# A CIN tower with 39 fields: layer 0's last pair tile as one float32r matmul

## The reference, cut to what matters

```python
prev = x                                          # [512, 39, 16]
for k in range(3):
    h = prev.shape[1]                             # 39, 128, 128
    z = jnp.einsum('bmd,bhd->bdmh', x, prev).reshape(b, D, m * h)
    t = jnp.einsum('bdc,co->bdo', z, ws[k]) + bs[k]      # co: o = 128
    t = jnp.transpose(t, (0, 2, 1))
    norm = jnp.sqrt(jnp.sum(t * t, axis=(-2, -1), keepdims=True))
    t = t / norm
    logit.append(t); prev = t
```

## Time and profile before

| | |
|---|---|
| median of 3 runs | 1101.58 us (1101.01 to 1102.05) |
| the profiled execution | 1101.28 us, span 1099.6 us |
| TensorE matmul busy | 96% |
| VectorE busy | 88% |
| GpSimd busy | 79% |
| ScalarE busy | 71% |
| mean DMA traffic | 37 GB/s |

### The profile page before, as it was taken

The page is one execution under the profiler, slowest core; times in us unless marked ns, Lnnn a source line. Parts: engine busy times, 40 slices in busy tenths (PEclk is TensorE's granted clock), DMA queues, the critical chain, the costliest instruction groups (busy, mean ns, idle before and its releaser), DMA issues.

```text
span 1099.6 us, 17904 instructions
## 1 busy us (share of the span) xinstructions
PE 1052.5 (96%) x4394; PEld 794.1 (72%) x4394; DVE 969.0 (88%) x3317; ACT 780.5 (71%) x2628; POOL 866.9 (79%) x726
## 2 busy tenths in 40 slices
PE   0798999999999999999999999999999999999999
PEld 0366687777778787777778777777777777788773
DVE  2467799998999999999999999999999999899892
ACT  3266586877768687776868777786868777688762
POOL 5587798888889888888888888888888888577660
PEclk9899999999999999999999999999999999999999
DMA  6503040110303011030303002030301203000000
GB/s 228 131 13 73 2 118 7 35 41 3 73 3 73 2 35 42 5 71 3 73 2 71 5 11 66 3 73 2 74 2 20 56 3 73 0 2 1 1 1 1
DMA packets 56735, 41.20 MB, mean 37 GB/s; under 512 B 37915, under 2 KB 40859, under 8 KB 56502
## 3 DMA queue, kind: packets, MB, share of 16 engines
q1 hardware_dynamic: 49145, 32.17, 12.5%
q10 hardware_dynamic: 2365, 6.60, 1.7%
q0 software_dynamic: 5120, 1.29, 1.3%
HBM read 38.09 MB, written 1.94 MB: 36 GB/s over the span
## 4 chain that ended last, share of the span: by engine, by line
PE 67%; POOL 21%; issue 6%; ACT 4%; DMA 1%; DVE 0%; SPq 0%; POOLq 0%; ACTq 0%
POOL sums L333 17%; PE bank_a L554 10%; PE bank_d L554 9%; PE acc L619 9%; PE bank_d L555 9%; PE bank_d L556 9%; PE bank_a L556 9%; PE bank_a L555 9%; POOL gathered L320 4%; ACT scaled L441 2%; PE turned L595 1%; ACT sums L441 1%; PE bank_a L684 1%; DMA x_pairs<-x_scratch 1%; PE bank_d L708 1%
## 5 line engine op out<-in xcount | busy, mean ns | idle before, releaser
L333 POOL TENSOR_TENSOR sums<-sums,scaled 128x512 f32<-128x512 f32 (+1 forms) x512 | 642.8, 1256 | 154.0 <-ACT scaled L441 119.3
L756 DVE SCALAR_TENSOR_TENSOR sums<-bank_d,x_col,sums 128x128 f32<-128x128 f32 x2304 | 654.8, 339 | 74.4 <-PE bank_d L556 58.8
L441 ACT ACTIVATE scaled<-bank_a,x_col 128x128 f32<-128x128 f32 x1920 | 550.6, 382 | 152.9 <-PE bank_a L556 144.4
L554 PE MATMUL bank_d<-w_hi,prev_lo 128*128 128x512 f32 x640 | 286.1, 447 | 1.2 <-DVE sums L775 0.9
L554 PE MATMUL bank_a<-w_hi,prev_lo 128*128 128x512 f32 (+1 forms) x640 | 274.5, 429 | 12.0 <-POOL prev_lo L338 6.3
L556 PE MATMUL bank_d<-w_hi,prev_hi 128*128 128x512 f32 x640 | 253.3, 396 | 0.0
L555 PE MATMUL bank_d<-w_lo,prev_hi 128*128 128x512 f32 x640 | 253.0, 395 | 0.0
L556 PE MATMUL bank_a<-w_hi,prev_hi 128*128 128x512 f32 (+1 forms) x640 | 246.2, 385 | 0.0
L555 PE MATMUL bank_a<-w_lo,prev_hi 128*128 128x512 f32 (+1 forms) x640 | 245.9, 384 | 0.0
L441 ACT ACTIVATE sums<-bank_a,x_col 128x128 f32<-128x128 f32 x512 | 146.1, 370 | 88.3 <-PE bank_a L556 88.3
L320 POOL DMA_INDIRECT gathered<-in_table,idx x160 | 177.2, 1107 | 31.9 <-issue 21.7
(11 more groups left out here) (59 smaller groups left out, 484.7 us busy)
## 6 DMA issues: line engine op xcount, KB each, us to landing
x_pairs<-x_scratch SPq DMA_DIRECT2D x141, 156.0 KB
x_pairs<-x_scratch SPq DMA_DIRECT2D x78, 78.0 KB
gathered<-in_table,idx POOLq DMA_INDIRECT x160
...
```

Source lines behind the costliest of these rows:

```text
L333: nc.gpsimd.tensor_tensor(out=sums[:, n % SUMS, 0:w, :], in0=sums[:, n % SUMS, 0:w, :], in1=scaled[:, a - 1, 0:w, :], op=ALU.add).then_inc ...
L441: op = nc.scalar.activation(to[:, i, :], bank_a[at % A_RING][:, i * UNITS:(i + 1) * UNITS], ACT.Copy, scale=x_of(c, q, a * PER_BANK + i))
L554: nc.tensor.matmul(to, lo, w_h, start=True, stop=False)
L756: nc.vector.scalar_tensor_tensor(out=taken(n, u) if u in LEFT else total, in0=taken(n, u), scalar=x_of(c, q, A_FIELDS + u), in1=total, op0 ...
```

## The change

The offsets 2 to 19 are 18 and fill six tiles of 117 rows. The 39 pairs with offset 1 go into the eleven rows 117 to 127 of the first four tiles (44 places; the five left over have zero weights). For them there are two copies of `x_rep`, one for group 0 and one for groups 1 and 2, each with its own eleven rows of fields, and eleven rows more in `x_rot`. Groups 0 and 1 have nine loads each, group 2 has three and group 3 none. For chunk 0 ScalarE's queue takes groups 1 and 2.

The 39 squares are computed on ScalarE (`square_x`) over three stacked copies, 117 rows, to `z0`, and copied to `z0s` as float32r. VectorE's operation of group 3 turns rows 78 to 116 of `z0s` into the low part, the square minus its float32r value; rows 0 to 77 keep the rounded value. The weights `w0s` are made once at the start, with the low part in rows 39 to 77. One float32r matmul of 117 rows thus sums high times high, high times low and low times high, in the place of the seventh tile. `low_rows` holds the factors 0 and -1, made by GpSimd at the start. The place of the squares on ScalarE is (0, 2) for chunk 1 and position 3 of the iteration's second job after that.

```diff
 OFFSETS = (FIELDS + 1) // 2
 PER_TILE = 128 // FIELDS
-PAIR_TILES = -(-OFFSETS // PER_TILE)
+PAIR_OFFSETS = list(range(2, OFFSETS))
+PAIR_TILES = len(PAIR_OFFSETS) // PER_TILE
 PAIR_ROWS = PER_TILE * FIELDS
-LAST_PAIR_ROWS = (OFFSETS - PER_TILE * (PAIR_TILES - 1)) * FIELDS
-PAIR_OFFSETS = list(range(1, OFFSETS)) + [0]
+EXTRA = 128 - PAIR_ROWS
+EXTRA_PAIRS = [(0, 0, 1, FIELDS - 1), (2, 2 * EXTRA, 2 * EXTRA + 1, 2 * EXTRA - 1)]
+SQUARES = PAIR_TILES
 PAIR_GROUPS = [[0, 1], [2, 3], [4, 5], [6]]
 NP = len(PAIR_GROUPS)
 SCRATCH_FIELDS = FIELDS + 5 * SLOT_FIELDS
...
         _summed = {(step_at(_it, 0), 5): [0], (step_at(_it, 0), 8): [1], (step_at(_it, 1), 1): [2],
                    (step_at(_it, 1), 4): [3], (step_at(_it, 2), 1): [4], (step_at(_it, 2), 4): [5],
                    (step_at(_it, 2), 8): [6]}
+    SQUARES_AT[(0, 2) if _it == 0 else (step_at(_it, 1), 3)] = _c
     PAIRS_AT.update({at: (_c, p) for p, at in enumerate(_made)})
     PAIR_MATMULS_AT.update({at: (_c, tiles) for at, tiles in _summed.items()})
...
 GATHERS_BEFORE = 3
 W2_FIRST, W2_SECOND = 3, 4
-SP_GROUPS, ACT_GROUPS = [0, 2], [1, 3]
+SP_GROUPS, ACT_GROUPS = [0], [1, 2]
 FEATURE_AT = [0, BATCH, 2 * BATCH + CB]
...
         base_sb = sb("base_sb", [128, GATHERS], i32)
         idx = sb("idx", [128, 2, GATHERS], i32)
         gathered = sb("gathered", [128, 2, GATHERS, EMB])
-        x_pairs = sb("x_pairs", [128, PAIR_TILES + 1, ROWS])
+        x_pairs = sb("x_pairs", [128, PAIR_TILES + 2, ROWS])
         x_rot = x_pairs[:, 0:PAIR_TILES, :]
-        x_rep = x_pairs[:, PAIR_TILES, :]
-        z0 = sb("z0", [128, PAIR_TILES, ROWS])
-        w0_sb = sb("w0_sb", [128, PAIR_TILES, UNITS])
+        x_reps = [x_pairs[:, PAIR_TILES + i, :] for i in range(2)]
+        x_rep = x_reps[0]
+        z0 = sb("z0", [128, PAIR_TILES + 1, ROWS])
+        w0_sb = sb("w0_sb", [128, PAIR_TILES + 1, UNITS])
+        z0s = sb("z0s", [PAIR_ROWS, ROWS], f32r)
+        w0s = sb("w0s", [PAIR_ROWS, UNITS], f32r)
+        low_rows = sb("low_rows", [128, 2])
         w0b_sb = sb("w0b_sb", [128, PAIR_TILES, UNITS])
         ones = sb("ones", [128, 128])
         identity = sb("identity", [128, 128])
...
         y_done = sem("y_done")
         y_stored = sem("y_stored")
-        PAIR_LOADS = [sum(PER_TILE * g[0] + kk < OFFSETS for kk in range(PER_TILE)) + (PER_TILE if g[0] == 0 else 0)
-                      for g in PAIR_GROUPS]
+        PAIR_LOADS = [2 * PER_TILE + 3, 2 * PER_TILE + 3, PER_TILE, 0]
         R_STEPS = 4
         def a_fields_of(a):
...
             rows = scratch[c, :, :].rearrange("(m b) e -> m (b e)", b=CB)
             tiles = PAIR_GROUPS[p]
+            def load(to, first, count, step):
+                at = rows[first:first + 1, :]
+                queue.dma_start(to, bass.AP(at.tensor, at.offset, [[step * ROWS, count], [1, ROWS]])
+                                ).then_inc(pairs_loaded[p], 16)
             for kk in range(PER_TILE):
                 at = slice(kk * FIELDS, (kk + 1) * FIELDS)
-                if p == 0:
-                    queue.dma_start(x_rep[at, :], rows[0:FIELDS, :]).then_inc(pairs_loaded[p], 16)
-                offsets = [PAIR_OFFSETS[PER_TILE * i + kk] for i in tiles if PER_TILE * i + kk < OFFSETS]
-                if offsets:
-                    first = rows[offsets[0]:offsets[0] + FIELDS, :]
-                    window = bass.AP(first.tensor, first.offset,
-                                     [[ROWS, FIELDS], [PER_TILE * ROWS, len(offsets)], [1, ROWS]])
-                    queue.dma_start(x_rot[at, tiles[0]:tiles[0] + len(offsets), :],
-                                    window).then_inc(pairs_loaded[p], 16)
+                if p < 2:
+                    load(x_reps[p][at, :], 0, FIELDS, 1)
+                first = rows[PAIR_OFFSETS[PER_TILE * tiles[0] + kk]:, :]
+                window = bass.AP(first.tensor, first.offset, [[ROWS, FIELDS], [PER_TILE * ROWS, len(tiles)], [1, ROWS]])
+                queue.dma_start(x_rot[at, tiles[0]:tiles[0] + len(tiles), :], window).then_inc(pairs_loaded[p], 16)
+            if p < 2:
+                tile, fields, *partners = EXTRA_PAIRS[p]
+                load(x_reps[p][PAIR_ROWS:128, :], fields, EXTRA, 2)
+                for i, partner in enumerate(partners):
+                    load(x_rot[PAIR_ROWS:128, tile + i, :], partner, EXTRA, 2)
         def bdim(ap):
             return ap.rearrange("p (b e) -> p b e", e=EMB)
...
                                         in1=prev_hi[k][:, c % 2, :].bitcast(f32),
                                         op=ALU.subtract).then_inc(prev_lo_made[k], 1)
+            nc.gpsimd.memset(low_rows[:, :], -1.0).then_inc(low_rows_set, 1)
+            for step, (col, base, sign) in enumerate(((0, -2 * FIELDS, 1), (1, -FIELDS, 1), (1, 2 * FIELDS - 1, -1))):
+                pool.wait_ge(low_rows_set, step + 1)
+                nc.gpsimd.affine_select(out=low_rows[:, col:col + 1], in_=low_rows[:, col:col + 1], pattern=[[0, 1]],
+                                        base=base, channel_multiplier=sign, compare_op=ALU.is_ge,
+                                        fill=0.0).then_inc(low_rows_set, 1)
             pool.wait_ge(ids_loaded, 32)
             make_rows(0)
             start_chunk(0)
...
                 if c:
                     sp.wait_ge(pairs_made, c * NP)
                     sp.wait_ge(x_turn_done, c)
-                for p in range(NP) if c else SP_GROUPS:
+                for p in range(NP - 1) if c else SP_GROUPS:
                     load_pairs(sp, c, p)
                 if c + 1 < CHUNKS:
                     store_chunk(c + 1)
...
                 nc.scalar.activation(x_col[:, c % 3, :, :], x_turned.rearrange("p (q m) -> p q m", m=FIELDS + 1),
                                      ACT.Copy).then_inc(x_col_made, 1)
+            def square_x(c):
+                act.wait_ge(pairs_loaded[0], (c + 1) * PAIR_LOADS[0] * 16)
+                if c:
+                    act.wait_ge(pairs_made, c * NP)
+                    act.wait_ge(pairs_summed, c)
+                nc.scalar.activation(z0[0:PAIR_ROWS, SQUARES, :], x_rep[0:PAIR_ROWS, :],
+                                     ACT.Square).then_inc(x_squared, 1)
+                act.wait_ge(x_squared, c + 1)
+                nc.scalar.activation(z0s[:, :], z0[0:PAIR_ROWS, SQUARES, :], ACT.Copy).then_inc(squares_hi_made, 1)
             def finish(k, c):
                 f = FINISH_NO[k, c]
                 if k == 0:
...
-            act.dma_start(w0_sb[0:PAIR_ROWS, :, :], w0a).then_inc(w0_loaded, 16)
-            act.dma_start(w0b_sb[0:PAIR_ROWS, :, :], w0b).then_inc(w0_loaded, 16)
+            act.dma_start(w0_sb[:, :, :], w0a).then_inc(w0_loaded, 16)
+            act.dma_start(w0b_sb[:, :, :], w0b).then_inc(w0_loaded, 16)
+            act.wait_ge(w0_loaded, 32)
+            nc.scalar.activation(w0s[:, :], w0_sb[0:PAIR_ROWS, SQUARES, :], ACT.Copy).then_inc(w0s_hi_made, 1)
...
                     scale_bank(A_BANKS * n + LEAD + a)
                     if (n, a) in TURN_COPIES_AT:
                         copy_x(TURN_COPIES_AT[n, a])
+                    if (n, a) in SQUARES_AT:
+                        square_x(SQUARES_AT[n, a])
                     for b, (_, _, at, _) in enumerate(NORMS):
                         if at == (n, a):
                             roots(b)
...
                     pe.wait_ge(squared, FINISH_NO[0, c - 1] + 1)
                 if tile == PAIR_GROUPS[group][0]:
                     pe.wait_ge(pairs_made, c * NP + group + 1)
-                rows = LAST_PAIR_ROWS if tile == PAIR_TILES - 1 else PAIR_ROWS
-                mm = nc.tensor.matmul(acc0[:, :], w0_sb[0:rows, tile, :], z0[0:rows, tile, :],
-                                      start=(tile == 0), stop=(tile == PAIR_TILES - 1))
-                if tile == PAIR_TILES - 1:
-                    mm.then_inc(pairs_summed, 1)
+                rows = 128 if tile <= EXTRA_PAIRS[-1][0] + 1 else PAIR_ROWS
+                if tile == SQUARES:
+                    nc.tensor.matmul(acc0[:, :], w0s[:, :], z0s[:, :], start=False, stop=True).then_inc(pairs_summed, 1)
+                else:
+                    nc.tensor.matmul(acc0[:, :], w0_sb[0:rows, tile, :], z0[0:rows, tile, :],
+                                     start=(tile == 0), stop=False)
             def norms(b):
                 items = NORMS[b][0]
...
             def make_pairs(c, p):
                 tiles = PAIR_GROUPS[p]
                 count = len(tiles)
+                if p == NP - 1:
+                    dve.wait_ge(squares_hi_made, c + 1)
+                    nc.vector.scalar_tensor_tensor(out=z0s[:, :], in0=z0s[:, :].bitcast(f32),
+                                                   scalar=low_rows[0:PAIR_ROWS, 0:1], in1=z0[0:PAIR_ROWS, SQUARES, :],
+                                                   op0=ALU.mult, op1=ALU.add).then_inc(pairs_made, 1)
+                    return
                 dve.wait_ge(pairs_loaded[p], (c + 1) * (PAIR_LOADS[p] * 16))
```

(17 more changed lines are left out.)

29 lines of the change are left out of this document (24 added, 5 removed).

## The result

| | before | after |
|---|---|---|
| median | 1101.39 us (1101.01 to 1102.45, 6 runs) | 1093.1 us (1092.3 to 1094.65, 6 runs) |
| the profiled execution | 1101.28 us, span 1099.6 | 1092.87 us, span 1090.9 |

The ratio is 0.9926, with a 95% interval from 0.9913 to 0.9939. The forecast was 1092.2 us: the time lies in the forecast's own range.

A forecast was written before the change was run, and what follows sets the result against it. TensorE's chain while layer-0 tiles last, then GpSimd's adds and gathers, were taken as the bound. Savings of 8.2 (chunks 3 to 15) + 0.5 + 0.63 + 0.1 = 9.4 us gave 1091.9, hence 1092.2; range 1090.0 to 1099.2.

The forecast's parts named there:

- The tile: TensorE's seventh tile per chunk: one float32r matmul of 0.23 us replaces two f32 instructions of 0.86, saving 0.63 us.
- The stretch: Job with the seventh tile, from one transpose of finished sums to the next: 7.8 us instead of 8.4.
- Rival (b): GpSimd's stretch swallows the saving, the meeting at 641.78 does not move: 1100.8 us; chance 10%.
- VectorE's product: VectorE's last product per chunk, 78x512 to 117x512: 0.67 us becomes 0.73, the added 0.06 hidden.
- Rival (a): VectorE's products and GpSimd's adds collide, giving back 0.3 us per chunk, 4.5 us: 1096.7; chance 19% with the like.
- ScalarE's pair: New Square and Copy on ScalarE's queue per chunk: about 1.4 us added, none of it reaching the path.
- rival (c): ScalarE's pair makes TensorE find its two-bank ring full, from 2.2 us on; at 3.3 us 1109; chance 7%.
- GpSimd's stretch as the bound: After layer-0 tiles GpSimd's adds and gathers pace jobs; the stretch starts sooner by TensorE's saving, up to 0.86 us.
- The start: Chunk 0's first loads, uncovered before the first transposes: group 0 lands 0.5 us later, 1.2 if all added bytes precede it.
- The rest of the start: ScalarE's splits of w1 slip some 2.6 us, GpSimd's memset and selections lie before 8.68; both cost nothing.
- Chunk 2's loads: Loads in the loop, 21 instead of 14 DMAs per chunk: hidden unless landing takes over 9 us.
- The tile of chunk 2: Chunk 2's seventh tile, half at the lower clock: saves 0.5 us (0.4 to 0.8).

The follow-up runs named there:

- experiment 1: Kernel before with only the seventh tile as one float32r matmul, low parts left out, no extra rows, nothing on ScalarE: 1090.98 us, ratio 0.9899.
- experiment 6: Changed kernel without TensorE's f32 matmul of tile 5 in every chunk but the first: 1082.99 us, ratio 0.9825.
- experiment 5: Changed kernel with ScalarE's Square and Copy done three times in every chunk but the first: 1128.33 us, ratio 1.0236.
- experiment 10: Changed kernel with chunk 0's group 2 loads back on SyncE's queue behind group 0, group 1 alone on ScalarE's: 1095.62 us, ratio 0.9934.
- experiment 8: The changed kernel as it is, timed and profiled once more in a later session: 1094.38 us, ratio 0.9924.
- ten fillers: Changed kernel with ten instead of three filling matmul rounds on TensorE ahead of the first transposes: 1092.03 us, ratio 0.9912.
- squares thrice: The run of experiment 5, ScalarE's Square and Copy three times in the changed kernel: 1128.33 us, ratio 1.0236.
- dealt and filled: Changed kernel with chunk 0's loads dealt over both queues, eight instead of three filling rounds before the transposes, two before tile 2: 1091.58 us, ratio 0.9902.
- group 0 first: Changed kernel with ScalarE's loads of groups 1 and 2 waiting until group 0 landed, its last three splits ahead of that wait: 1093.98 us, ratio 0.992.
- group 2 with 0: The run of experiment 10, chunk 0's groups 0 and 2 on SyncE's queue in the changed kernel: 1095.62 us, ratio 0.9934.

## Why the forecast held, and where it was off

**The tile: right.** 0.63 us per chunk were forecast; step 14 shows 0.64, experiment 1 alone 0.61. With 0.05 of another step that the forecast didn't have, 13 chunks brought 9.0 us instead of 8.2. The stretch was to be 7.8 and is 7.71, an iteration 62.5 and is 62.5. Rival (b), by which GpSimd's stretch swallows the saving, fell with it.

**VectorE's product: right**, 0.73 us in the trace and 0.77 in the mean. Rival (a) fell: the adds do run long beside it (4.49 us for three from 625.10, where three take 4.18 us in the row of experiment 6), yet every step but the one with the tile kept its length.

**ScalarE's pair: right in kind, over-priced.** It takes 1.22 us, not 1.4: the hand-off is 0.03 us (622.68 + 0.65 to 623.36), not 0.1, and each operation is 0.65 rather than 0.71. The point of rival (c) was put at 2.2 us and is 1.98, with a slope of one; the slope holds only as long as TensorE's clock does. With a wait of 1.6 to 1.8 us ten iterations of fourteen pay the 1.9, and four, in which the clock falls, pay 3.5 (experiment 5).

**GpSimd's stretch as the bound: wrong, without harm.** The forecast read the chain of waits, 21% GpSimd, as two regimes, and allowed the saving only up to GpSimd's idle 0.86 us. The saving was smaller than that, so the sum came out; for a saving of 1.49 us (experiment 6 with the change) the reading would have lost 0.6 us an iteration that the chip gave in full. The windows pointed to TensorE all along: in each of the three jobs TensorE's busy time equals the length of the job, the third included, and no other engine's does in all three. In the first VectorE's does too, so that a full window names candidates, and experiment 6 had to tell which of them sets the length. The chain follows releases, and it can go back through GpSimd's adds where TensorE would have come to the same place by its own work.

**The start: the step that failed.** The forecast had group 0 land 0.5 us later, "+0.5", bound 1.2. Its load takes 2.3 us longer (11.5 for 9.2) and begins 0.5 later. The beginning varies from 25.8 to 27.4 over the twelve profiles, whatever the kernel. The length does not: it is 11.3 to 12.2 in the six profiles with the changed kernel's loads, and 9.2 and 8.8 in the two with the old ones. Two things were wrong. The 0.5 us that group 2's move was to bring is not there (experiment 10). And the bound counted the bytes added, 0.21 MB, where it had to count the bytes that land ahead of the last of group 0: by the windows 9.2 us at 178 GB/s are 1.64 MB before, 11.5 us at 169 GB/s are 1.94 MB after. By estimate 1.7 of the 2.3 us are those 0.30 MB at 178 GB/s, and 0.6 the lower rate; why the rate is lower was not tried. VectorE's products show the same thing: before, the third waited 0.18 us more for its loads; after, all three of groups 0 to 2 run in one piece behind 38.19.

Less than 2.8 us of it reached the path. The tiles ran faster in the changed kernel (6.82 us for twelve instructions and one float32r, where fourteen took 8.55), which left 1.3 us at ScalarE's bias of chunk 0, behind the last tile (46.65 for 45.37); another 0.6 us went in the waits between there and transpose 0, which is 0.65 us late. How fast they run varies from run to run by 1.1 us (experiment 8), and with it the start's term.

**The rest of the start: right at nothing.** ScalarE's splits of w1 began 1.4 us later (12.63 for 11.26), not 2.6, and VectorE's first use of them did not move (21.91 for 22.04). GpSimd made `low_rows` by 1.7 us, ahead of its next work at 8.48.

**Chunk 2's loads: not hidden.** The forecast covered the loads of the loop with 9 us of lead. That is so from iteration 2 on. In iteration 1, where the queue starts them at 96.54, the first product at 103.45 waits for them; 0.49 us of it reach step 4. In the kernels that come to transpose 3 within 7.9 to 8.1 us of these loads' first issue (ten fillers, squares thrice, dealt and filled, group 0 first, group 2 with 0) 1.3 us reach it (11.64 for 10.33); in those that take 8.8 us or more nothing does. The tile of chunk 2 was put at 0.5 us (0.4 to 0.8). Step 6, which holds it, is 0.95 us shorter in this profile (11.89 for 12.84) and 0.2 in the same program's second one (12.66), so no run shows this term by itself. Chunk 1's saving of 0.63 us is not seen in step 2 (12.63 for 12.41), a step that spreads from 12.45 to 13.87 over the eleven kernels of the table that have the shorter tile.

**The account.** Forecast: 8.2 (chunks 3 to 15) + 0.5 + 0.63 + 0.1 = 9.4. Measured in the profiles: 9.0, less 0.3 for all up to transpose 12, is 8.7 at the last transpose and in the span, 8.4 in the profiled executions' times. The two misses, 0.8 more in the loop and 1.5 less at the start, have opposite signs, so that only 0.7 us is seen of them; that part of the agreement is luck. The -0.3 of the start is also no better known than the 1.6 us by which two profiles of the changed kernel differ at transpose 12.
